# Order of the first loads and of the cross attention's first steps in a one-layer decoder kernel

## What is computed

```python
# attention over the 4*256 tokens: 16 query heads, 4 key/value heads of 128, rope, window of 128
q, k, v = rope(x @ q_kernel), rope(x @ k_kernel), x @ v_kernel
x = layernorm(x + softmax(mask(q @ k.T / sqrt(128))) @ v @ out_kernel)
# cross attention: its attention matrix needs ctx (4, 256, 128) and two 128x128 weights only
query = ctx @ Wq.T + bq
key   = ctx @ Wk.T + bk
attention = softmax(query @ key.T)
x = layernorm(x + x @ attention.T)
# feed forward: 2 shared experts and 16 routed ones of width 176, top 4 gates
x = layernorm(x + shared(x) + sum_e gate_e(x) * expert_e(x))
```

## Time and profile before

| | us |
|---|---|
| median of 3 runs | 456.1 |
| lowest, highest | 454.03, 456.33 |
| the profiled execution, its span | 457.5 |
| TensorE busy | 406.4 (89%) |
| VectorE busy | 308.9 (68%) |
| ScalarE busy | 267.0 (58%) |
| GpSimd busy | 168.3 (37%) |

### The profile page before, as it was taken

How to read it: one execution, slowest core, us unless ns; L and a number is a source line. 1 busy time by engine, 2 the same in 40 slices (tenths; PEclk the granted TensorE clock), 3 DMA queues, 4 the chain that set the end, 5 groups by cost and what they waited for, 6 DMA issues and landing times.

```text
span 457.5 us, 8275 instructions
## 1 busy us (share of the span) xinstructions
PE 406.4 (89%) x2297; PEld 343.3 (75%) x2297; DVE 308.9 (68%) x851; ACT 267.0 (58%) x659; POOL 168.3 (37%) x288
## 2 busy tenths in 40 slices
PE   3977898999889999899998896884899999999992
PEld 2766787999779988789997674561788888888871
DVE  1685999797987889887889745440655555555545
ACT  3566977785657775567774631610655555555553
POOL 0142656553664556535646402010222232222210
PEclk9986999999999999999999996997799999999997
DMA  6511230000000000000002950035433333333302
GB/s 225 198 47 47 91 116 25 3 0 2 1 1 23 0 0 0 0 0 0 0 0 60 327 183 0 0 44 99 113 92 95 100 96 91 96 100 94 90 10 92
DMA packets 20716, 29.29 MB, mean 64 GB/s; under 512 B 1305, under 2 KB 15794, under 8 KB 20696
## 3 DMA queue, kind: packets, MB, share of 16 engines
q1 hardware_dynamic: 20696, 29.05, 22.9%
HBM read 27.19 MB, written 1.86 MB: 63 GB/s over the span
## 4 chain that ended last, share of the span: by engine, by line
PE 67%; DVE 16%; issue 7%; DMA 4%; ACT 2%; POOL 2%; SPq 1%; POOLq 0%; DVEq 0%; ACTq 0%
PE bank L524 18%; PE bank L525 17%; PE bank L526 17%; PE bank L608 4%; PE bank L617 2%; PE bank L580 2%; PE bank L607 2%; DMA gates_d<-gatesT 2%; DMA gate_rows<-gates_d 1%; DVE by_sin L1047 1%; DVE by_cos L1046 1%; PE bank L574 1%; DVE scores L1057 1%; DVE xln L1118 1%; PE bank L680 1%
## 5 line engine op out<-in xcount | busy, mean ns | idle before, releaser
L1002 DVE TENSOR_TENSOR hid<-hid,gate_rows 128x512 f32<-128x512 f32 (+1 forms) x46 | 32.0, 699 | 68.8 <-ACT hid L810 50.8
L810 ACT ACTIVATE hid<-bank,b_cols 128x512 f32<-128x512 f32 (+1 forms) x50 | 34.3, 687 | 42.1 <-PE bank L526 42.1
L1286 POOL TENSOR_SCALAR nprobs<-probs,rsums 128x128 f32<-128x128 f32 x64 | 24.0, 375 | 91.6 <-DVE rsums L1064 86.2
L1293 POOL TENSOR_TENSOR w_lo<-w_raw,w_hi 128x256 fp32r<-128x256 f32 (+1 forms) x25 | 20.7, 829 | 89.6 <-ACT w_hi L802 89.6
L1278 POOL TENSOR_TENSOR queryT<-by_cos,by_sin 128x512 f32<-128x512 f32 x32 | 42.5, 1328 | 28.8 <-DVE by_sin L1047 27.8
L524 PE MATMUL bank<-hid_hi,w_hi 128*128 128x512 f32 (+1 forms) x100 | 40.1, 401 | 8.2 <-DVE hid_lo L989 8.0
L989 DVE TENSOR_TENSOR hid_lo<-hid,hid_hi 128x512 fp32r<-128x512 f32 (+1 forms) x50 | 39.3, 819 | 5.7 <-ACT hid_hi L819 3.1
L870 ACT COPY swapped<-bank 64x512 f32<-64x512 f32 x40 | 23.3, 583 | 32.6 <-PE bank L526 32.4
L524 PE MATMUL bank<-x2T_hi,w_hi 128*128 128x512 f32 (+1 forms) x100 | 40.5, 405 | 0.5 <-DVE xln L1031 0.5
L524 PE MATMUL bank<-xT_hi,wq_hi 128*128 128x256 f32 x128 | 38.8, 303 | 1.7 <-issue 1.2
L525 PE MATMUL bank<-x2T_lo,w_hi 128*128 128x512 f32 (+1 forms) x100 | 40.1, 401 | 0.0
(11 more groups left out here) (174 smaller groups left out, 1176.5 us busy)
## 6 DMA issues: line engine op xcount, KB each, us to landing
gate_rows<-gates_d SPq DMA_DIRECT2D x22, 512.0 KB
w_raw<-in_L_ffn_routed_w SPq DMA_DIRECT2D x2, 1408.0 KB, 8.2
w_raw<-in_L_ffn_routed_w SPq DMA_DIRECT2D x1, 2688.0 KB, 12.5
stage<-in_L_attn_q_kernel SPq DMA_DIRECT2D x4, 512.0 KB, 6.3
stage<-in_L_attn_out_kernel SPq DMA_DIRECT2D x4, 512.0 KB, 3.5
xb<-in_x SPq DMA_DIRECT2D x4, 256.0 KB, 2.9
res<-in_x SPq DMA_DIRECT2D x1, 1024.0 KB, 6.2
out<-x SPq DMA_DIRECT2D x8, 128.0 KB, 1.8
```

What stands on the lines that cost most here:

```text
L810: nc.scalar.activation(hid[0:n, par, h * HALF:(h + 1) * HALF], bank[2 + 2 * par + h][0:n, :], ACT.Relu, bias=b1_cols[0:n, bass.ds(c, 1)]). ...
L1002: nc.vector.tensor_tensor(hid[0:n, par, cols], hid[0:n, par, cols], gate_rows[0:n, par, cols], ALU.mult).then_inc(gated, 1)
L1286: nc.gpsimd.tensor_scalar(nprobs[:, u, 0:W], probs[:, u, 0:W], rsums[:, u, 0:1], 1.0, ALU.mult, ALU.mult)
```

## The change

```diff
-PIECE_AT = dict(zip(PIECE_NAMES, (-2.1, -2.05, -0.9, 2.2, 3.1, 5.4, 6.6, 8.1, 10.1, 12.1)))
+PIECE_AT = dict(zip(PIECE_NAMES, (-2.45, -2.4, -0.9, 2.2, 3.1, 5.4, 6.6, 8.1, 10.1, 12.1)))
 ONCE_AT = {
-    "pe": {"ctx turned": -2.4, "ctx projected": -2, "energy 0": -0.9, "energy 1": -0.85,
+    "pe": {"ctx turned": -1.2, "ctx projected": -0.95, "energy 0": -0.9, "energy 1": -0.85,
...
-    "act": {"ctx turned": -2.35, "ctx projected": -2, "e_exp 0": -0.3, "e_exp 1": -0.25,
+    "act": {"ctx turned": -1.2, "ctx projected": -0.95, "e_exp 0": -0.3, "e_exp 1": -0.25,
...
-    "dve": {"ctx turned": -2.35, "ctx projected": -1.95, "e_top 0": -0.7, "e_top 1": -0.65,
+    "dve": {"ctx turned": -1.2, "ctx projected": -0.95, "e_top 0": -0.7, "e_top 1": -0.65,
...
             sp.dma_start(ident[:], ident_c).then_inc(ld_ident, 16)
-            sp.dma_start(xw[:, 0, :], xwq).then_inc(ld_ctx, 16)
-            sp.dma_start(xw[:, 1, :], xwk).then_inc(ld_ctx, 16)
-            sp.dma_start(xb_cols[:, 0:1], xbq.rearrange("(d a) -> d a", a=1)).then_inc(ld_ctx, 16)
-            sp.dma_start(xb_cols[:, 1:2], xbk.rearrange("(d a) -> d a", a=1)).then_inc(ld_ctx, 16)
-            sp.dma_start(ctx_sb[:], ctx_v).then_inc(ld_ctx, 16)
             for n in range(4):
                 sp.dma_start(stage_view(n), PIECES[n][0]).then_inc(ld_stage[n % 4], 16)
                 if n == 1:
+                    sp.dma_start(xw[:, 0, :], xwq).then_inc(ld_ctx, 16)
+                    sp.dma_start(xw[:, 1, :], xwk).then_inc(ld_ctx, 16)
+                    sp.dma_start(ctx_sb[:], ctx_v).then_inc(ld_ctx, 16)
+                    sp.dma_start(xb_cols[:, 0:1], xbq.rearrange("(d a) -> d a", a=1)).then_inc(ld_ctx, 16)
+                    sp.dma_start(xb_cols[:, 1:2], xbk.rearrange("(d a) -> d a", a=1)).then_inc(ld_ctx, 16)
                     sp.dma_start(cos_t[:], cos_c).then_inc(ld_tables, 16)
```

## The result

The changed kernel took 459.27 us (median of 20 runs, 455.53 to 461.56), the kernel before 456.69 (20 runs beside them, 453.95 to 459.36). The ratio is 1.0056, 95% interval 1.0034 to 1.0078: slower by 1.6 to 3.6 us. The forecast of 454.6 missed with its range and its sign.

The account below looks back on a forecast made before the run. The first 24 us were taken as TensorE's serial run behind the context's transfer. Terms summed to 1.9 us gained (early clock rise) or 0.8 (late); 1.5 was taken, from 456.1 to 454.6 us, range 452.0 to 457.2.

Parts of the forecast that it names:

- The landing: First query weights, loaded behind x and identity, land at 5.6 us, so slot q0 starts at 8.0 instead of 16.2.
- bytes in order: Load queue: landings priced by adding up bytes in issue order, each landing 1.0 to 1.2 us behind its last byte.
- the columns: Bias columns, small packets, last of the cross attention's loads: land at 9.6 us; rival of late inputs at 12.8, 457.4, chance 0.08.
- the late rise: TensorE's clock rises 6.4 us after slot q0 starts, at 14.4; 0.8 us gained, 455.3, chance 0.20.
- the early rise: TensorE's clock rises 3.1 us after slot q0 starts, at 11.1; projections start at 13.8, 1.9 us gained.
- The cover: Key copy no longer runs beside slots q0 and k0, so the energies wait for it behind the projections: +0.8 us.
- Copy, projections, key addition: Context's second-half copy right behind q0's rope, near 13; projections 3.45 us; key addition, 2.20 us before, well shorter.
- the mark: Start of VectorE's rope of q1, 24.04 us before, forecast between 22.2 and 23.6; all later work should move with it.
- one low stretch more: Rival: TensorE's longer pause before the first turned attention makes the clock fall, +0.6 to 2.2 us, up to 456.8; chance 0.10.
- one stretch less: Rival: one of two 1.2 GHz stretches between 31.85 and 45.17 us drops out, 2.2 us less, 452.4; chance 0.22.
- The side: Whole time against a 0.5% threshold: chance 0.31 below 453.8, 0.65 between, 0.04 above 458.4.
- the late case: Sum of the beginning's steps with the clock rising at 14.4: projections start at 14.9, q1's rope at 23.55 us.

Follow-up runs that it names:

- e3_q0_alone: Changed kernel with every load behind the first query weights issued only once these have landed; they landed at 6.25 us, no whole time given.
- e4_columns_last: Changed kernel with the two bias columns loaded behind the mask, on a semaphore of their own; ratio 1.0045 to the kernel before.
- e8: Changed kernel with 6 idle matmuls in TensorE's pause ahead of slot q0; ratio 1.0006 to the kernel before, 458.39 us.
- e11: Changed kernel with 24 idle float32 transposes in TensorE's pause ahead of slot q0; 457.94 us in one run.
- e15: Changed kernel with energies behind slot q1, 3, 4 and 3 idle matmuls ahead of the turned attentions, 8 ahead of slot q0; ratio 0.9902, 452.89 us.
- e7_cover: Changed kernel with the energies of batches 0 and 1 behind slot q1 instead of ahead of it; ratio 0.9994 to the kernel before.
- e6_fill_after: Changed kernel with 11 idle matmuls (4, 4 and 3) in TensorE's pauses ahead of the turned attentions; ratio 0.9985 to the kernel before.
- e14_fill3_changed: Changed kernel with 3, 4 and 3 idle matmuls in TensorE's pauses ahead of the turned attentions; ratio 0.9988 to the kernel before.
- e9_cover_fill: Changed kernel with energies behind slot q1 and 3, 4 and 3 idle matmuls ahead of the turned attentions; ratio 0.9934 to the kernel before, 454.93 us.
- e12_changed_again: Changed kernel run again unchanged, beside the same runs of the kernel before; ratio 1.0042.

## Why the prediction was wrong

**The landing, the step that failed.** "0.52 MB of query weights at 390 GB/s take 1.35 us, so they land at 3.15 + 1.35 + 1.1 = 5.6 us." It landed at 7.29 to 8.42 in the changed kernel's two profiles. Two things in this step failed. The first is the rate: I took the 390 of a queue that has run for 8 us, although show 167 and 168 in the slices from 3.0 on, in the old order as well. At the 184 GB/s that the changed kernel shows from 3.0 to 6.0 the same sum gives 7.1. The second is bytes in order: alone in the queue the piece landed at 6.25 (e3_q0_alone), 0.65 behind my 5.6, and with the other loads behind it 0.9 to 2.1 later than that, so what is queued behind a load does delay it here. I read the low rates of 4.0 to 5.5 us as the columns' doing; e4_columns_last shows that the late landing isn't. The upper bound (6.4) was wrong for the same reason: it is the length of a load that had begun later. Slot q0 started at 9.71 to 10.82 for 8.0, which by my own words broke the step. The tables, said to land at 11.0, landed at 12.8 in the changed kernel, and at 13.0 to 13.8 in e8, e11 and e15, where VectorE waits for them; the mask's issue, which was to keep its 6.25, came at 7.68.

**The clock.** The projections were to start at 13.8 or 14.9; they started at 16.43. 1.7 of this is the landing. The rest is the late rise, which the prediction had as a rival of 0.20: but that rival had another reason, that transposes don't count, and e11_warm_transposes shows that they do. Why it took 5.7 us here and 3.2 in e7_cover is open; e6_fill_after and e14_fill3_changed show that it isn't the program, since the same beginning gave an earlier rise there. No row decided for the early rise, to which I leaned.

**The cover.** The wait of 0.8 was there, at 0.94. What was mis-sized is its weight, since I set it off against gains elsewhere and didn't ask what it would be worth to avoid it. In e7_cover it is, with the early rise of that execution, 2.7 us at the rope of q2 and about 2.3 in the time; in the fairer pair, e9_cover_fill against e14_fill3_changed, 2.3 (2.2 with the landings set equal) and about 2.5.

**Copy, projections, key addition.** The wait ahead of the turning went, the copy stood right behind the rope of q0 (15.14, not 13), the projections took 3.45 as said, and the key addition took 1.27 for 2.20. Mechanisms right, all later by the landing.

**Mark and span.** Later work did follow the mark, as said: 1.56 at the mark, 1.1 from the rope of q2 to 60 us, 1.3 at the end. In e12_changed_again it is 2.6, 2.2 and 2.2. A mean landing at 7.9 instead of 7.29 is between the two profiles.

**The low stretches.** The rival "one low stretch more" (0.10) named the pause ahead of the turned attention, 1.63 to become 2.6. It became 2.59, and the share of executions at 0.960 or 0.961 rose from 7% to 53%. But the length of that pause isn't the whole cause: in e7_cover it is 1.64 again, and all ten executions are at 0.960 or 0.964. What decides is open. The rival that I gave more, one stretch less (0.22), went the other way: the executions of the changed kernel at 0.967 or more are 25%, where before they were 58%.

**The side.** Slower by over 0.5% had 0.04 and only one mechanism, the columns. The one term on which all of the gain stood, an early first landing, had bounds of 5.1 and 6.4 from loads that ran later in the queue; there was no rival on it. A landing at 7.29 alone, put into my sum, moves the late case from 23.55 to 25.2; less the 0.3 that is 0.9 us lost, about 457. The 459.27 needs the lower clocks behind 30 us as well.

## What to carry to other kernels

The first microseconds of a load queue are not like the rest: price a load at the head of the program by the rates of these very slices, and not by the rate that the queue reaches later. When a step is pulled ahead, look at what it covered; the energies one slot later were worth as much as the whole change lost. And where TensorE waits, a few matmuls that nobody reads can be worth as much as a better order: on the changed kernel with its cover back the ratio fell from 0.9994 to 0.9934 with those in the pauses behind 28 us, and to 0.9902 with those ahead of the first slot, which is some 2.7 and 1.5 us (1.9 and 2.0 by the medians). In the kernel before, most of whose executions have a higher mean clock anyway, those in the pauses gave only 0.7 and 1.5 us.

## What the runs showed of the hardware

The landing of one and the same first load spread from 7.1 to 8.4 us over nine profiles of kernels with the same loads. Alone in the queue it landed at 6.25. Float32 transposes raised TensorE's clock as matmuls did: in e11_warm_transposes their records shorten from 0.42 to 0.27 us, and slot q0 behind them ran at 0.12 us a matmul from its start. With one and the same beginning the rise came 5.7 us after the first matmul of slot q0 in one execution and inside the turning in another. The time of the kernel before lies in lumps by its mean granted clock, 456.4, 457.9 and 459.2 us. In the changed kernel, whose pause ahead of the turned attention is 1 us longer, other lumps are the frequent ones, and by the shares alone that is 1.1 us.
